# Attention with a mixture of experts on one core: two transposing DMAs, one for each half of the probabilities, and TensorE takes the high half's products first

## The reference

```python
q = q.reshape(B, S, NUM_HEADS, HEAD_DIM)
...
scores = jnp.einsum('bqhd,bkhd->bhqk', q, k) / jnp.sqrt(jnp.float32(HEAD_DIM))
attn = jax.nn.softmax(scores, axis=-1)
out = jnp.einsum('bhqk,bkhd->bqhd', attn, v).reshape(B, S, NUM_HEADS * HEAD_DIM)
return _mxfp4_matmul(out, wo_codes, wo_scales) + bo
...
x = x + _layernorm(_L0_attn_ref(_layernorm(x, axis=-1), ...), axis=-1)
x = x + _layernorm(_L0_ffn_ref(_layernorm(x, axis=-1), ...), axis=-1)
```

## Time and profile before

| what | us |
|---|---|
| median of 3 runs | 1362.71 |
| lowest and highest | 1360.33, 1367.67 |
| the profiled execution's own time | 1350.27 |
| its span, first to last instruction | 1348.4 |

### The profile page before, as it was taken

One profiled execution on the slowest core, in us unless ns is written; L12 is line 12 of the kernel. 1 busy time (PEld: TensorE's weight loads), 2 busy tenths in 40 slices (PEclk: granted clock), 3 DMA queues, 4 the chain that ended last, 5 costly groups with the idle time before them and its releaser, 6 DMA issues.

```text
span 1348.4 us, 25270 instructions
## 1 busy us (share of the span) xinstructions
PE 1208.2 (90%) x7836; PEld 850.9 (63%) x7836; DVE 875.3 (65%) x2285; ACT 826.2 (61%) x2128; POOL 926.6 (69%) x1126
## 2 busy tenths in 40 slices
PE   2798989999999999989999999998959999999984
PEld 1465666666666666656666666665635677778863
DVE  5789567687768758777876876777667322232247
ACT  2566668777777777777777677767745332233413
POOL 2898556568877886886888798788764733444553
PEclk9999999999999999999999999999999999899978
DMA  6684796745555445454544444443445489887683
GB/s 227 144 212 112 183 240 157 167 96 122 122 105 111 88 103 98 76 95 94 91 76 90 90 80 85 77 82 66 94 100 163 150 228 241 202 231 204 133 256 125
DMA packets 364678, 182.68 MB, mean 135 GB/s; under 512 B 287440, under 2 KB 343222, under 8 KB 364544
## 3 DMA queue, kind: packets, MB, share of 16 engines
q1 hardware_dynamic: 344960, 166.18, 52.2%
q0 software_dynamic: 16416, 11.70, 4.8%
q10 hardware_dynamic: 3168, 3.15, 0.7%
HBM read 75.32 MB, written 64.69 MB: 104 GB/s over the span
## 4 chain that ended last, share of the span: by engine, by line
PE 41%; DVE 20%; DMA 12%; POOL 11%; issue 8%; ACT 5%; SPq 1%; POOLq 0%; ACTq 0%; DVEq 0%
PE bank L1038 8%; PE bank L1009 7%; DMA PT<-PH 7%; PE bank L1053 7%; DMA Y<-W,wix 5%; PE bank L1024 4%; PE bank L1070 4%; POOL P L940 4%; POOL PH L945 3%; PE bank L1178 3%; DVE nm L1413 3%; POOL BUF L700 3%; PE bank L1191 3%; DVE O L1419 2%; PE bank L1102 2%
## 5 line engine op out<-in xcount | busy, mean ns | idle before, releaser
L940 POOL TENSOR_SCALAR P<-P,rr 128x256 f32<-128x256 f32 x512 | 250.0, 499 | 141.9 <-DVE rr L1409 135.2
L1274 ACT ACTIVATE P<-bank,nm 128x256 f32<-128x256 f32 x512 | 237.6, 469 | 151.8 <-DVE nm L1413 145.5
L945 POOL TENSOR_TENSOR PH<-P,PH 128x512 f16<-128x512 f32 x256 | 295.7, 1169 | 17.7 <-ACT PH L1283 16.9
L1009 PE MATMUL bank<-RB,W 128*128 128x512 f16 x1076 | 256.1, 380 | 8.7 <-ACT Sx L629 4.3
L700 POOL DMA_INDIRECT BUF<-RT,ix x192 | 199.0, 1036 | 84.1 <-issue 41.2
L1038 PE MATMUL bank<-RB 128*128 128x256 f32 x1024 | 246.7, 384 | 4.0 <-issue 2.2
L1053 PE MATMUL bank<-PT,RB 128*128 128x256 f16 x1536 | 197.1, 273 | 35.4 <-DMA PT<-PH 32.2
L1413 DVE TENSOR_REDUCE nm<-bank 128x2 f32<-128x512 f32 x256 | 174.7, 683 | 54.4 <-PE bank L1038 53.9
L1053 PEld LDWEIGHTS bank<-PT,RB 128*128 128x128 f16 x1536 | 145.5, 98 | 94.1 <-DMA PT<-PH 48.1
L1038 PEld LDWEIGHTS bank<-RB 128*128 128x128 f32 x1024 | 186.6, 192 | 27.8 <-issue 4.0
L1283 ACT ACTIVATE PH<-P 128x512 f16<-128x512 f32 x256 | 161.4, 631 | 52.9 <-POOL P L940 36.5
(11 more groups left out here) (200 smaller groups left out, 1614.4 us busy)
## 6 DMA issues: line engine op xcount, KB each, us to landing
RB<-in_ewT SPq DMA_DIRECT2D x24, 352.0 KB
BUF<-zrow SPq DMA_DIRECT2D x4, 1926.0 KB, 8.7
W<-BUF SPq DMA_DIRECT2D x64, 120.4 KB, 4.3
HT<-in_ewT SPq DMA_DIRECT2D x18, 352.0 KB
HT<-in_wc SPq DMA_DIRECT2D x24, 256.0 KB, 4.8
HT<-in_ws SPq DMA_DIRECT2D x24, 256.0 KB, 5.2
Y<-zrow SPq DMA_DIRECT2D x10, 512.0 KB, 3.6
RB<-in_ewd SPq DMA_DIRECT2D x24, 176.0 KB
```

The source lines that it names most:

```text
L940: r = eng.tensor_scalar(p, p, rr[:, w % 4, t:t + 1], SP_, ALU.mult, ALU.mult)
L945: eng.tensor_tensor(PH[:, w % 2, 1, :], P[:, w % 2, :], PH[:, w % 2, 0, :], ALU.subtract).then_inc(s["pl"], 1)
L1009: r = eng.matmul(bk_[:, :], W[:, m, a, c * 2048 + h * 128:c * 2048 + (h + 1) * 128], XT[:, bp % 2, b, c, :], start=(k == 0), stop=(k == n ...
L1274: r = eng.activation(P[:, u % 2, t * 256:(t + 1) * 256], bS[u % 2][:, t * 256:(t + 1) * 256], ACT.Exp, bias=nm0[:, u % 4, t:t + 1], accum_ ...
```

## The change

The one DMA of a unit becomes two, of four blocks each. The first waits for `ph` and the free buffer and signals `s_pt`; the second waits for `pl` and signals a new semaphore, `s_pu`. Both are issued by SyncE, in its one queue. TensorE takes the four products with the high half first, then waits for `s_pu` and takes the two with the low half; they are the same six products. `p_high` waits for the high half's DMA of unit w-2 alone, and `p_low` waits for the low half's.

```diff
@@ turn_p
-                eng.wait_ge(s["pl"], w + 1)
+                eng.wait_ge(s["ph"], w + 1)
                 if w >= 2:
                     eng.wait_ge(s["pv"], w - 1)
-                eng.dma_start_transpose(PT[:, w % 2, :, :, :, :].rearrange("p l t c q -> p (l t c) q"),
-                                        PH[:, w % 2, :, :].rearrange("p l n -> p (l n)")).then_inc(s_pt[w % 2], 16)
+                eng.dma_start_transpose(PT[:, w % 2, 0, :, :, :].rearrange("p t c q -> p (t c) q"),
+                                        PH[:, w % 2, 0, :]).then_inc(s_pt[w % 2], 16)
+                eng.wait_ge(s["pl"], w + 1)
+                eng.dma_start_transpose(PT[:, w % 2, 1, :, :, :].rearrange("p t c q -> p (t c) q"),
+                                        PH[:, w % 2, 1, :]).then_inc(s_pu[w % 2], 16)
@@ p_low
                 eng.wait_ge(s["ph"], w + 1)
+                if w >= 2:
+                    eng.wait_ge(s_pu[w % 2], 16 * (w // 2))
@@ pv
-                for kc in range(2):
-                    for a, b in PASS:
-                        r = eng.matmul(bO[:, q * 256:(q + 1) * 256],
-                                       V[:, i // 4 % 2, a, 2 * q + kc, h % 4 * 128:(h % 4 + 1) * 128],
-                                       PT[:, u % 2, b, :, kc, :], start=(k == 0), stop=(k == 5))
-                        k += 1
+                for b, kc, a in ((0, 0, 0), (0, 0, 1), (0, 1, 0), (0, 1, 1), (1, 0, 0), (1, 1, 0)):
+                    if k == 4:
+                        eng.wait_ge(s_pu[u % 2], 16 * (u // 2 + 1))
+                    r = eng.matmul(bO[:, q * 256:(q + 1) * 256],
+                                   V[:, i // 4 % 2, a, 2 * q + kc, h % 4 * 128:(h % 4 + 1) * 128],
+                                   PT[:, u % 2, b, :, kc, :], start=(k == 0), stop=(k == 5))
+                    k += 1
```

More of the change, by code:

```diff
@@ L344, in build @@
         s_pt = [sem(f"s_pt{i}") for i in range(2)]
+        s_pu = [sem(f"s_pu{i}") for i in range(2)]
         s_x1 = [sem(f"s_x1{i}") for i in range(2)]
@@ L862, in _ @@
                 eng.wait_ge(s_pt[k], 16 * NI)
+                eng.wait_ge(s_pu[k], 16 * NI)
             eng.wait_ge(s["pv"], NU)
```

## The result

| | before | after |
|---|---|---|
| median of the runs, us | 1362.51 (1360.33 to 1367.67, 4 runs) | 1380.88 (1379.39 to 1385.86, 4 runs) |
| ratio, 95% interval | | 1.0126 [1.0096, 1.0156] |
| profiled execution: span, us | 1348.4 | 1377.6 |
| last `PV` of the attention begins, us | 996.1 | 1014.8 |

The changed kernel takes 18.4 us more, where the prediction had 13 us less. The profiled spans differ by more, 29.2 us. The 19 us up to the last `PV` (18.7 as they stand in the table, 19.8 counted from the first `PV` of each trace) are what has to be explained.

A forecast was written before the change was run, and what follows sets the result against it. TensorE's work was taken to set the period; 20 chain pieces, 0.7 us shorter each, gave 14 us, less 1 us for new waits: 13 us off the median, 1349.7 us. Most likely 1349.5 us, bounds 1335 to 1370.

The forecast's parts named there:

- What bounds the kernel: In mid-attention TensorE works 94 of every 100 us and sets a pair's period; it stands 32.2 us for transposes before `PV`.
- Half a transpose, data: On the DMA engines, a half moves in 0.7 us instead of 1.4 and lands about 2.35 us after its issue begins.
- Half a transpose, issue: On SyncE's queue, issuing a half takes 0.82 us, between 0.62 and the 1.24 of a whole.
- 20 pieces, each 0.4 to 0.8 us shorter, 14 us: Transposing-DMA pieces on the chain that ended last, 91.2 us together, shorten by 0.7 us each, saving 14 us.
- The earlier start: In an undisturbed pair the even high half starts at 395.8, not 396.39, making the odd unit ready 0.4 us earlier.
- at 1.24 us it is a loss of 0.8 us: On the odd unit's path, an issue costs three times its difference: gain 1.0 us at 0.62, nothing at about 0.95.
- Where another DMA stands between: Where a store sits between even and odd transposes, 0.8 us of TensorE's 1.34 us wait before odd `PV` is saved.
- ScalarE's `p_high`: It waited 0.62 us for the whole DMA in one pair; needing only the high half, its wait is nearly gone.
- GpSimd's new wait in `p_low`, costed at nothing: `p_low` waits for a low half issued a pair earlier, which lands before `p_low` begins; cost nothing.
- TensorE's second wait and the order: In `PV`, 256 new waits cost at most 0.02 us each; 0 to 1 us taken in all.
- The rival that came true: On SyncE's queue, a half's issue costs as much as a whole's: 20 to 35 us lost, 1390 us; chance 0.17.
- The page weighed in the prediction: DMA advice to coalesce small transfers spoke against the cut, making the gain about 7 us; the trace was preferred.

The follow-up runs named there:

- p1_issue_probe: Kernel before with the new product order, plus 18 lone transposes of 1 to 16 blocks behind the attention; one block took 1.14 us to issue, eight 1.23.
- e6_whole_at_fill: Changed kernel with units 24 to 33 each transposed whole by one DMA; 1364.62 us beside 1347.84 for the kernel before, ratio 1.0128.
- e3_no_pool_wait: Changed kernel with three low-half buffers instead of two, so `p_low` need not wait; 1370.52 us beside 1348.98 for the kernel before, ratio 1.0161.
- e1_order_only: Kernel before with only TensorE's product order changed, one DMA a unit, no second wait; 1349.2 us beside 1351.42, ratio 0.9994.
- v3_4_8_4: Changed kernel with the even low and odd high halves merged, three DMAs a pair; 1346.24 us beside 1351.42 for the kernel before, ratio 0.9968.
- e7_quarters: Changed kernel with each half cut again, four DMAs of two blocks a unit; 1827.48 us beside 1353.13 for the kernel before, 35% slower.

## Why the prediction was wrong, step by step

- **What bounds the kernel** was right: TensorE's work sets the period, the clock is at its level of 2.4 GHz in the attention but for the 3.4 us stretches above, which the prediction left out, and TensorE's wait for these DMAs before `PV` is what moved the time, in the other direction (32.2 to 47.0 us).
- **Half a transpose, data**: right. Predicted 0.7 us of data and a landing 2.35 us after the issue begins; measured about 0.7 us and 2.4 to 2.5.
- **Half a transpose, issue**: this is the step that failed. "The 0.8 us on top, for a transpose, would halve. I take 0.82 us": it is 1.21 and 1.27 us, and one block costs 1.14. The trace of before had one size of transpose only, so it couldn't tell a price per DMA from a price per block. I took the store's 0.53 us as the fixed part and gave the rest to the blocks. The probe shows that the rest doesn't go with the blocks: from eight to one it falls by 0.1 us. So the term "20 pieces, each 0.4 to 0.8 us shorter, 14 us" of the sum had the wrong sign.
- **The earlier start**, computed from that price: 0.4 us earlier was predicted for the odd unit. The text's own rule, "at 1.24 us it is a loss of 0.8 us", holds nearly: 1.3 us of slack before the odd unit's first reader became 0.3 before its fifth matmul, a loss of 1.0. With 20 pieces on the chain the rule would have given 16 us of loss, near the 18.4; that is partly luck, as the undisturbed pairs have the slack to lose nothing and 5.9 us are lost in four pairs at the zero fills.
- **Where another DMA stands between**: 0.8 us less was predicted for such pairs. Some of them are among those that lose, as the pair at 386 us, with a store between its transposes and a wait of 1.98 us. At the zero fills the whole transposes take the step away in the trace (`e6_whole_at_fill`); where the other steps come from wasn't tested. The pair at 433 us has no other DMA of SyncE between its issues, and waits for a late landing.
- **ScalarE's `p_high`** was to wait no more. It still waits 14.1 us in 11 waits between 170 and 1000 us, where it had 12.9 in 14 before.
- **GpSimd's new wait in `p_low`, costed at nothing**: it waits (11.5 us in all), and costs nothing, as `e3_no_pool_wait` shows. Right in the cost, though the reason given, that the low half has landed by then, doesn't hold in 14 waits.
- **TensorE's second wait and the order**, 0 to 1 us: the order costs nothing (`e1_order_only`); the waits weren't measured alone, and `v3_4_8_4`, which has one for every unit and is faster than before, leaves no room for a large price.
- **The rival that came true** is the third: the issue of a half costs as much as a whole. Its mechanism and its condition (above 0.95 us an issue) held. Its price, "a third of 128 pairs lose 0.5 to 0.8 us", 20 to 35 us, was a little too high: 18.4 us in the medians, and 5.9 of the 19.8 us in the trace are lost in four pairs and not in a third of them. It had 0.17.
- **The page weighed in the prediction**: the Trainium skill, "DMA: Bandwidth & Descriptors", section "Rules for kernel authors", advises to coalesce small transfers. The Trainium skill speaks there of transfers under 64 KB, and a half has 128. In direction the runs agree: twice the DMAs for the same bytes cost 1.3%, four times cost 35%, and merging two of the four halves (`v3_4_8_4`) turns the loss into a gain. The prediction held that rule against the time of a half's data, which did shrink as the trace had it, and not against the issuing queue, where it counts.

Open: what holds an issue at 2 to 3 us where other DMAs are under way, and how much of the loss there is SyncE's and how much the full DMA engines' (no run issues the halves from another engine); what makes the steps outside the zero fills; why cutting the odd unit alone costs as much as the even one; why what is won at the zero fill is partly lost again by the end.

## What to carry to other kernels

Before a DMA is cut in two, count the issues of a period on the queue and price them by the DMA and not by the byte, unless the trace has two sizes of the same kind; here it had one, and the price turned out constant up to eight blocks. A count alone doesn't decide: three issues a pair were 0.65 and 0.87% slower or 0.3% faster, by what they let start and land early. Look at the places where the queue carries other DMAs, since an undisturbed period has the slack that these places lack. Cut only where the early part is waited for, and merge the neighbours that are ready at the same time, so that the number of issues grows least: 4, 8 and 4 blocks gave 0.3% where 4, 4, 4 and 4 cost 1.3%.

## What the runs showed of the hardware

- A transposing DMA of fp16 from SyncE, with nothing else of its kind under way (`p1_issue_probe`, medians of three, and for sixteen the least and the most), holds the engine for 1.14 us with one block of 128 by 128, 1.18 with two, 1.19 with four, 1.23 with eight, 1.43 with twelve and 1.9 to 2.8 with sixteen. Up to eight it is a price per DMA; above that it grows.
- An issue behind a large DMA takes longer: 1.58 us in the median for four blocks behind twelve, 1.6 to 2.9 us for four blocks at the zero fills.
- A DMA lands when the last of its 16 parts does, and one can be late by itself: of the half issued at 433.01 us 15 parts had landed by 436.7 and the last at 438.2, with a mean DMA share of 0.05 from 436 to 437 us. A scatter of GpSimd's had been issued at 433.09, and between 436.5 and 437.2 us the only packets with data are two of the queue that takes GpSimd's DMAs (2.6 and 5.1 KB); whether they stood in the way wasn't tried.
- After a wait TensorE can run at the lower of its two levels for 3.4 us: eight matmuls of the scores took 3.12 us at 394.39 and 1.89 at 402.12.
- In `e7_quarters` TensorE was busy for 76% of the span, and the mean of its granted clock was 0.883, where it was 90% and 0.978 before. From its first `PV` to its last, 1417 us, it spent 369 at the lower of its two levels (1.2 and 2.4 GHz), where before it spent 7 of 945. How much of the 35% that costs isn't separated; the queue's 10.7 of the 11.1 us of a pair leave little room for it.
